# One Trainium2 kernel: the last token tile's down projection, norm and store in two column halves, and each final norm moved ahead of the next tile's sum

## What is computed

```
def _bitlinear(x, w):
    scale = jnp.mean(jnp.abs(w))
    q = jnp.round(jnp.clip(w / (scale + EPS), -1.0, 1.0))
    return x @ (q * scale).T
...
gate = _bitlinear(x, w_gate)
up = _bitlinear(x, w_up)
out = _bitlinear(gate * up, w_down)          # 1376 -> 512 features
x = _layernorm(x + out, axis=-1)             # over the 512 features, then stored
```

## Time and profile before

| | |
|---|---|
| median of 3 runs | 480.82 us (480.57 to 481.75) |
| the profiled execution's own time | 480.79 us |
| its span, first to last instruction | 478.9 us |
| PE busy, share of the span | 463.3 us, 97% |
| DVE busy | 336.8 us, 70% |
| ACT busy | 259.7 us, 54% |
| POOL busy | 233.3 us, 49% |
| mean granted clock of TensorE | 0.999 of full |

### The profile page before, as it was taken

The page is one execution under the profiler, slowest core; times in us unless marked ns, Lnnn a source line. Parts: engine busy times, 40 slices in busy tenths (PEclk is TensorE's granted clock), DMA queues, the critical chain, the costliest instruction groups (busy, mean ns, idle before and its releaser), DMA issues.

```text
span 478.9 us, 6373 instructions
## 1 busy us (share of the span) xinstructions
PE 463.3 (97%) x2068; PEld 369.1 (77%) x2068; DVE 336.8 (70%) x579; ACT 259.7 (54%) x508; POOL 233.3 (49%) x285
## 2 busy tenths in 40 slices
PE   7999999999999969999999999999999999999995
PEld 7887777876777748888878888888887777788883
DVE  3673876655587677676799899984877665587274
ACT  4889857777656656655423344222708665658000
POOL 6474555527553468767877300026028455652022
PEclk9999999999999999999999999999999999999999
DMA  7720222021222314525313336620200010000022
GB/s 239 247 88 4 86 89 66 22 89 47 75 79 91 129 42 156 184 87 192 119 58 132 133 108 205 214 90 0 85 4 0 0 46 24 1 0 1 0 89 88
DMA packets 14432, 40.81 MB, mean 85 GB/s; under 512 B 2368, under 2 KB 2368, under 8 KB 14400
## 3 DMA queue, kind: packets, MB, share of 16 engines
q1 hardware_dynamic: 14400, 40.41, 25.2%
HBM read 38.30 MB, written 2.10 MB: 84 GB/s over the span
## 4 chain that ended last, share of the span: by engine, by line
PE 85%; DVE 5%; ACT 5%; issue 2%; POOL 2%; POOLq 0%; DVEq 0%
PE psA L1712 7%; PE psA L1714 7%; PE psA L1727 4%; PE psA L1729 4%; PE psA L1718 3%; PE psA L1720 3%; PE psB L1923 3%; PE psB L1919 3%; PE psB L1922 3%; PE psA L1700 2%; PE psA L1705 2%; PE psA L1701 2%; PE psB L2010 2%; PE psB L2011 2%; PE psB L2022 2%
## 5 line engine op out<-in xcount | busy, mean ns | idle before, releaser
L796 POOL TENSOR_SCALAR var<-mv 128x1 f32<-128x1 f32 x16 | 4.5, 280 | 108.0 <-DVE mv L1293 107.9
L858 POOL TENSOR_TENSOR beta<-wsum,beta 128x512 fp32r<-128x512 f32 x28 | 36.2, 1312 | 24.5 <-ACT beta L1060 24.5
L1182 ACT ACTIVATE c<-c 128x512 f32<-128x512 f32 x14 | 8.9, 633 | 46.9 <-DVE c L1519 46.9
L1700 PE MATMUL psA<-xT_h,win_h 128*128 128x512 f32 x80 | 32.5, 407 | 0.0
L1701 PE MATMUL psA<-xT_l,win_h 128*128 128x512 f32 x80 | 31.4, 393 | 0.0
L1419 DVE SCALAR_TENSOR_TENSOR xbc<-psA,convw_sb,xbc 128x511 f32<-128x511 f32 (+2 forms) x36 | 26.9, 747 | 4.4 <-ACT xbc L1119 3.6
L1192 ACT ACTIVATE act_hl<-act 128x512 fp32r<-128x512 f32 x28 | 16.9, 627 | 17.1 <-PE psB L1923 10.9
L1712 PE MATMUL psA<-xT_h,beta 128*128 128x512 f32 x56 | 22.4, 401 | 1.0 <-issue 0.7
L984 POOL TENSOR_TENSOR int_l<-int,int_h 128x512 fp32r<-128x512 f32 x11 | 14.3, 1298 | 18.1 <-ACT int_h L1263 18.1
L1714 PE MATMUL psA<-xT_l,beta 128*128 128x512 f32 x56 | 21.9, 391 | 0.0
L1705 PE MATMUL psA<-xT_h,win_l 128*128 128x512 f32 x80 | 21.9, 395 | 0.0
(11 more groups left out here) (336 smaller groups left out, 1591.5 us busy)
## 6 DMA issues: line engine op xcount, KB each, us to landing
raw<-in_f_gu_t SPq DMA_DIRECT2D x22, 512.0 KB, 3.4
raw<-in_w_gu_t SPq DMA_DIRECT2D x14, 512.0 KB, 3.7
raw<-in_f_dn_t SPq DMA_DIRECT2D x10, 512.0 KB, 3.4
raw<-in_w_gu_t SPq DMA_DIRECT2D x14, 256.0 KB, 2.9
raw<-in_w_dn_t SPq DMA_DIRECT2D x7, 512.0 KB, 3.9
raw<-in_w_in_t SPq DMA_DIRECT2D x5, 512.0 KB, 4.0
x<-in_hidden SPq DMA_DIRECT2D x8, 256.0 KB, 5.1
out<-x SPq DMA_DIRECT2D x8, 256.0 KB, 2.0
```

The lines of the kernel that those rows point to most:

```text
L858: nc.gpsimd.tensor_tensor(beta[:, f % 2, 1, cols], wsum[:, f % 2, cols], beta[:, f % 2, 0, cols].bitcast(F32), ALU.subtract).then_inc(gb_l ...
L1700: nc.tensor.matmul(ps, sh, mh, start=i == 0, stop=False)
```

## The change

It has three parts.

1. In the list of steps, for batch 1, `("ln2", 1, c - 1)` now stands between `("ffndown1", c)` and `("ffnsum", 1, c)`, not behind it.
2. PE computes the last tile (`("ffndown1", 3)`) by halves of its columns: 22 matmuls over columns 0 to 255 in the bank of job `("ffndown", 1, 3)`, then 22 over columns 256 to 511 in that of a new job `("ffndown", 1, 4)`. Each half raises `b_done`. DVE adds each half and takes its statistics as it comes (two halves in the two slots of `bn6`), and aggregates both at the end.
3. The last tile's normalisation on DVE and its store by SP are each in two halves.

```diff
@@ build_schedule
     for c in range(NC):
-        steps += [("ffndown1", c), ("ffnsum", 1, c)]
-        if c >= 1:
-            steps.append(("ln2", 1, c - 1))
+        steps += [("ffndown1", c)] + ([("ln2", 1, c - 1)] if c else []) + [("ffnsum", 1, c)]
     steps.append(("ln2", 1, NC - 1))
@@ psum_jobs
         elif kind == "ffndown1":
-            b.append(("ffndown", 1, *at))
+            b += [("ffndown", 1, *at)] + ([("ffndown", 1, NC)] if at[0] == NC - 1 else [])
@@ layer_kernel
+        halves_of_tile = [slice(0, D // 2), slice(D // 2, D)]
@@ SP
-            for t in range(NT):
+            for t in range(NT - 1):
                 sp.wait_ge(out_ready, t + 1)
                 sp.dma_start(out[t], x[:, t, :]).then_inc(out_stored, 16)
-            sp.wait_ge(out_stored, 16 * NT)
+            for i, cols in enumerate(halves_of_tile):
+                sp.wait_ge(out_ready, NT + i)
+                sp.dma_start(out[NT - 1, :, cols], x[:, NT - 1, cols]).then_inc(out_stored, 16)
+            sp.wait_ge(out_stored, 16 * (NT + 1))
@@ DVE
+                elif step == ("ffnsum", 1, NC - 1):
+                    t = tile_of(step)
+                    v.wait_ge(ln1_ready, t + 1)
+                    for i, cols in enumerate(halves_of_tile):
+                        job = ("ffndown", 1, at[1] + i)
+                        v.wait_ge(*done_b(job))
+                        nc.vector.scalar_tensor_tensor(out=x[:, t, cols], in0=bank_b(job)[:, cols],
+                                                       scalar=scl[:, 13:14], in1=x[:, t, cols], op0=ALU.mult,
+                                                       op1=ALU.add).then_inc(half_summed, 1)
+                        v.wait_ge(half_summed, i + 1)
+                        v.wait_ge(bn_ready, NT + t)
+                        link(nc.vector.bn_stats(bn6[:, i, :], x[:, t, cols]))
+                    nc.vector.bn_aggr(mv[:, NT + t, :], bn6[:]).then_inc(bn_ready, 1)
...
                     v.wait_ge(rstd_ready, i + 1)
-                    nc.vector.tensor_scalar(x[:, t, :], x[:, t, :], mv[:, NT + t, 0:1], rstd[:, i:i + 1],
-                                            ALU.subtract, ALU.mult).then_inc(out_ready, 1)
+                    for cols in halves_of_tile if t == NT - 1 else [slice(0, D)]:
+                        nc.vector.tensor_scalar(x[:, t, cols], x[:, t, cols], mv[:, NT + t, 0:1], rstd[:, i:i + 1],
+                                                ALU.subtract, ALU.mult).then_inc(out_ready, 1)
@@ PE
+                elif step == ("ffndown1", NC - 1):
+                    c = at[0]
+                    for i, cols in enumerate(halves_of_tile):
+                        ps = open_b(("ffndown", 1, c + i))
+                        for f in range(FF):
+                            high, low = int_parts(1, f)
+                            nc.tensor.matmul(ps[:, cols], high[:, chunk(c)], q_dn[:, f, cols], start=f == 0,
+                                             stop=False)
+                            done = nc.tensor.matmul(ps[:, cols], low[:, chunk(c)], q_dn[:, f, cols], start=False,
+                                                    stop=f == FF - 1)
+                        done.then_inc(b_done, 1)
```

More of the change, by code:

```diff
@@ L562, in layer_kernel @@
         bn_ready = sem("bn_ready")
+        half_summed = sem("half_summed")
         ln1_ready = sem("ln1_ready")
```

## The result

| | before | changed |
|---|---|---|
| median of 12 runs each | 480.88 us | 481.82 us |
| span of the profiled execution | 478.9 us | 479.7 us |
| start of the last tile's first matmul | 467.92 | 467.92 |
| from there to the end of the span (called the tail below) | 10.98 us | 11.78 us |

The ratio of the runs is 1.0021, with a 95% interval of 1.0013 to 1.0028: the changed kernel is 0.6 to 1.3 us slower, which is 0.2% and under the 0.3% from which the prediction would speak of a difference. The prediction was 481.3 us, +0.5, in a range of 480.5 to 482.6.

A forecast was written before the change was run, and what follows sets the result against it. PE was taken to bound the kernel as a whole, but the change to touch only the last 11 us. Second store's issue +0.83, less 0.30 for its transfer, gave +0.5: 481.3 us, range 480.5 to 482.6.

The forecast's parts named there:

- DVE's rhythm: Batch 1 on DVE: rounds of 3.105 us as in batch 0, so DVE is free for the last tile at 473.54.
- PE's price and its cover: Last tile on PE: 44 matmuls at 0.120 us, 5.28 for 4.99; the extra hidden with 1.11 us of cover.
- DVE's halves: Last tile on DVE: half-sum 0.48, statistics 0.43; aggregate at 475.48 (+0.86), norm at 476.61 (+0.66).
- Norm and store by halves: Last tile's end: half norm 0.37, second store issues at 477.35 (+0.83), smaller transfer saves 0.3; sum +0.5 us.
- As laid out: Rival, last tile: DVE free when the first half is done, hiding it under PE's second; -0.6, 480.2 us; chance 0.05.
- Costly halves: Rival, PE's second half: short matmuls cost more than half, 0.188 or 0.2267 us each; 483.1 or 484.8 us; chance 0.08.
- The 0.214 us for a pair: Last tile on PE: weight load and short matmul in series, 0.107 + 0.107 by the skill's rules; estimate 484.2 us.

The follow-up runs named there:

- two padded kernels: Changed kernel with 8 or 16 extra transposes on PE between the last tile's two halves; tails 11.79 and 12.51 us, against 11.78 in the changed kernel.
- e4: Kernel before, last tile's matmuls and sums halved, third tile's norm between the half-sums, last norm and store whole; ratio to before 0.9993, tail 10.58 us.
- e6 with 8: Changed kernel with 8 extra transposes on PE between the last tile's two halves; span 480.6 us, tail 11.79 us.
- e8: Changed kernel with PE's second half of the last tile in two quarters of 128 columns; span 481.5 us, tail 12.97 us.
- e10: Kernel before with only batch 1's third tile's norm moved ahead of the last tile's sum; ratio to before 0.9989, tail 10.80 us.

## Why the prediction was right

**DVE's rhythm** was right to 0.02 us: the third norm at 473.06 for 473.08 expected, the first half-sum at 473.52 for 473.54. The order alone shows that this is the cause, and the halves alone that the first half is hidden without it. One reading was off: four norms in a row waited 0.95 us for POOL before the change, not five; the fifth that waited is the last of all, with 0.71.

**PE's price and its cover** were right: 0.120 us a matmul, and PE's extra 0.29 us unseen. The two padded kernels show the cover and where it ends. The reasoning for the 0.120 (a fixed 0.013 on each float32r matmul on top of its columns) was lucky: it fits 256 columns, but at 128 the distance is 0.112, and not 0.067. Near 256 columns a floor is close, and the sum of columns and fixed part just came out above it. The 0.013 is not what its rows give either: 0.2267 less half of 0.42 is 0.016, which would have made 0.121.

**DVE's halves** were right: 0.48 and 0.43, aggregate at 475.48, last norm at 476.63 for 476.61.

**Norm and store by halves** is the term that was mis-sized. The second store issued at 477.45, +0.93 for the +0.83 of the sum. Of these 0.10, 0.02 come from the norm's later start, 0.05 lie between it and the first store (the half norm takes 0.41 and not 0.37), and 0.03 between the two stores' issues (0.38 apart, for 0.35). The smaller transfer gave back 0.13 (2.38 - 2.25) and not 0.3; against the changed kernel with a whole store it is 0.20 (2.45 - 2.25). So part 3 made the sum +0.8 and not +0.5. The section "Anatomy of one DMA" of the Trainium skill, "DMA: Bandwidth & Descriptors", which stands beside the 0.3, describes DMAs that GpSimd issues. SP issues these stores, and the trace decides. The profiled spans differ by exactly these 0.8 us, and the runs' interval of +0.6 to +1.3 holds it, but not the +0.5.

**The range** has a slip. Its lower end is the median less 0.1 and 0.25, as its sentence says; by the same sentence the upper end would be 480.82 + 1.3 + 0.9 = 483.0, and not 482.6. The 481.82 lies inside either, so nothing hangs on it here.

**The rivals.** *As laid out* did not come, and would have been worth little: with the old order the halves give 0.05 us. It was put at -0.6; the halves with the third norm between come to -0.37, and the missing 0.2 is the norm and store again. *Costly halves* did not come, though a floor of the kind that it feared is there, at 0.112 instead of 0.188. The 0.214 us for a pair, an estimate by two rules of the Trainium skill ("TensorE: Matmul & The Clock Gate"), has no support in the 0.120 and 0.112 of these runs. The rule that fails is the one on overlap: all these loads and matmuls use the full 128 x 128 array, and the loads run beside the matmuls all the same. The section that holds it, "The mechanism", also lets a load into the background weight buffer go ahead of matmuls in flight, which these distances would fit. The other rule, 107 ns for a load, lies just under the 0.112 and is not contradicted.

## What to carry to other kernels

A consumer that waits in each round for a third engine's answer gets its own rhythm; putting its second step behind the next item's first step is what hides that wait, and taking it back is right only for the item at which the consumer idles anyway. Splitting the last item pays only if the consumer is free when the first part comes, so look at what ends the idle time before the last item's first instruction. A chain of small steps behind the last matmul can be worth more than the width of the vector operations around it: here a shorter way through 128 numbers gave 0.35 us (tails 10.58 and 10.23), and the halves 0.22.

## What the runs showed of the hardware

An instruction of POOL on 128 numbers took 0.39 us where DVE normalised a tile beside it, and 0.19 alone; moving that norm took 0.2 us off the chain in three kernels (the order alone, the norm between, one norm moved).

Most of the scatter between the executions profiled here, which hides effects of this size, is made in the first 9 us. The same 30 transposes that open PE's work give way to the first real ones at 7.83 to 9.05 us. In eleven of the twelve profiles the last tile's first matmul follows that moment by 459.65 to 459.90 us, whatever the moment was. The rows show PE in windows of 1 us before the change, and then in the kernel with the order alone (window, its length, busy time with the number of matmuls, granted clock, DMA share, GB/s):

```profile
6.00:7.00 1.00, 1.00 (x7) 1.00 0.94 248
7.00:8.00 1.00, 1.00 (x11) 1.00 0.82 105
```

```profile
7.00:8.00 1.00, 1.00 (x7) 1.00 0.45 62
8.00:9.00 1.00, 1.00 (x8) 1.00 0.89 198
9.00:10.00 1.00, 1.00 (x11) 1.00 0.96 369
```

The rate goes from 7 matmuls a microsecond to 11 in both, 1 to 2 us later in the second, and that execution is 0.76 us behind when the last tile starts. The profile's granted clock reads full in all of these windows, so these rows don't say what changes there. The kernel with the deviation through ACT is the twelfth and does not fit: it is 0.16 us early after these transposes and 0.35 us late at the last tile, and why is open.

A lower clock in the middle of the kernel did not show in the end. In e4 the granted clock reads 0.50, which is the level of 1.2 GHz, for some 3.4 us from 171.7 on. PE idles from 170 to 171 before it, but it does so in the kernel with the order alone as well, whose clock stays full there. The rows are e4's:

```profile
170.00:171.00 1.00, 0.00 (x0) 1.00 0.00 0
171.00:172.00 1.00, 0.71 (x3) 0.87 0.00 0
172.00:173.00 1.00, 1.00 (x4) 0.50 0.00 0
```

The last tile starts 459.81 us after the opening transposes, and 459.71 before the change, where the clock stays full in this stretch. PE has idle time there to catch up in: before the change it is busy for 0.38 of the microsecond from 174 and 0.01 of that from 178. The same dip stands in three more profiles (e6 with 8, e8, e10).
